# The recurrent layer's finish moved into the cross attention behind it, and batches 1 to 3 turned and projected between the first scores

## The reference, cut to what matters

```
xn = layernorm(x)
r  = scan_output(xn) + xn
x  = x + (layernorm(r) * gamma + beta)      # end of the recurrent sublayer
h  = layernorm(x)                           # x2 begins
q  = h @ Wq + bq ;  k, v = ctx @ Wk, ctx @ Wv ;  s = mask(q k^T / sqrt(8)) ...
```

## Time and profile before

| | |
|---|---|
| runs, median of 3 | 2433.44 us (2431.93 to 2447.59) |
| the profiled execution | 2440.75 us, its span 2438.9 us, mean granted TensorE clock 0.889 |
| PE matmul busy | 2066.0 us (85% of the span) |
| PE weight loads busy | 1383.0 us (57%) |
| DVE busy | 1662.4 us (68%) |
| ACT busy | 1045.7 us (43%) |
| POOL busy | 533.2 us (22%) |

### The profile page before, as it was taken

The page is one execution under the profiler, slowest core; times in us unless marked ns, Lnnn a source line. Parts: engine busy times, 40 slices in busy tenths (PEclk is TensorE's granted clock), DMA queues, the critical chain, the costliest instruction groups (busy, mean ns, idle before and its releaser), DMA issues. The chain is left out here.

```text
span 2438.9 us, 36556 instructions
## 1 busy us (share of the span) xinstructions
PE 2066.0 (85%) x12192; PEld 1383.0 (57%) x12216; DVE 1662.4 (68%) x4273; ACT 1045.7 (43%) x2326; POOL 533.2 (22%) x905
## 2 busy tenths in 40 slices
PE   6698899998999897767774997598699979999888
PEld 3455788884555455433332554587334348777777
DVE  5666677786675576779997565456679856666655
ACT  2354222222564453455551344322367734444333
POOL 0342110102110530068883321010211010000010
PEclk8698899997897799889996798799689979999989
DMA  8321000004120420000003220000511110000000
GB/s 338 99 60 23 1 1 1 1 1 130 44 53 18 121 60 2 1 1 0 1 1 105 73 48 8 1 1 1 174 36 46 33 44 1 1 1 1 1 1 18
DMA packets 60073, 94.61 MB, mean 39 GB/s; under 512 B 11313, under 2 KB 33137, under 8 KB 58737
## 3 DMA queue, kind: packets, MB, share of 16 engines
q1 hardware_dynamic: 29312, 55.29, 6.7%
q0 software_dynamic: 29952, 36.45, 6.2%
q10 hardware_dynamic: 624, 0.54, 0.1%
HBM read 65.50 MB, written 31.29 MB: 40 GB/s over the span
## 5 line engine op out<-in xcount | busy, mean ns | idle before, releaser
L1008 DVE TENSOR_REDUCE m<-banks 128x1 f32<-128x512 f32 (+3 forms) x512 | 272.6, 584 | 94.6 <-PE banks L1172 54.4
L2687 PEld LDWEIGHTS banks<-w_ffn,eh 128*128 128x128 f32 x2144 | 279.2, 191 | 23.5 <-DVE eh L2628 1.9
L2687 PE MATMUL banks<-w_ffn,eh 128*128 128x128 f32 x2144 | 281.2, 274 | 1.5 <-DVE eh L2628 1.5
L1140 ACT ACTIVATE p<-banks 128x512 f32<-128x512 f32 (+3 forms) x512 | 234.0, 522 | 101.4 <-PE banks L1218 58.7
L1443 DVE TENSOR_REDUCE m<-banks 128x2 f32<-128x308 f32 x384 | 165.7, 475 | 137.1 <-PE banks L1743 70.3
L2675 PE MATMUL banks<-x_hi,w_hi 128*128 128x512 f32 x472 | 211.2, 447 | 17.4 <-PEq L332 17.4
L1170 PE MATMUL banks<-K,Qf 32*128 32x512 f32 (+2 forms) x512 | 182.5, 515 | 14.6 <-PEq L332 9.9
L2657 ACT ACTIVATE et<-banks 128x512 f32<-128x512 f32 x140 | 83.6, 597 | 246.8 <-PE banks L2677 203.2
L2677 PE MATMUL banks<-x_hi,w_lo 128*128 128x512 f32 x472 | 188.7, 400 | 0.0
L2676 PE MATMUL banks<-x_lo,w_hi 128*128 128x512 f32 x472 | 187.6, 397 | 0.0
L1216 PE MATMUL banks<-Q,K 32*128 32x512 f32 (+2 forms) x512 | 153.5, 499 | 14.9 <-ACT p L1140 13.0
(11 more groups left out here) (423 smaller groups left out, 4332.7 us busy)
## 6 DMA issues: line engine op xcount, KB each, us to landing
Qf<-stack_q_plain POOLq DMA_DIRECT2D x48, 256.0 KB, 3.0
Qf<-stack_q_masked POOLq DMA_DIRECT2D x32, 256.0 KB, 3.0
K<-stack_k_self POOLq DMA_DIRECT2D x32, 256.0 KB, 3.1
w_ffn<-ffn_dram SPq DMA_DIRECT2D x1, 6144.0 KB, 35.2
stack_q_plain<-q_hi SPq DMA_DIRECT2D x24, 256.0 KB, 3.1
stack_q_masked<-q_hi SPq DMA_DIRECT2D x16, 256.0 KB, 3.0
stack_k_self<-k_hi SPq DMA_DIRECT2D x16, 256.0 KB, 3.8
K<-stack_k_ctx POOLq DMA_DIRECT2D x48, 80.0 KB, 2.7
```

Of the source, the lines that this page charges most:

```text
L1008: ins = dve.reduce_max(k.m[:, t, h:h + 1], bank[:, 0:(t + 1) * P if k.kind == "page" else S], AX)
L1140: nc.scalar.activation(k.p[:, x % PBUFS, q0:S], score_banks[x % 3][:, q0:S], ACT.Exp).then_inc(sem("exp_done"), 1)
L2687: last = pe.matmul(bank[:, t * P:(t + 1) * P], k.h[:, n % RING, t * P:(t + 1) * P], w(down.format(e))[:, i * P:(i + 1) * P], start=(i == 0 ...
```

## The change

The finish. `scan_finish` and its block are gone. x2 is called with `finish=True`, which counts as `early = 0`. POOL adds beta batch by batch at the start of the x2 block, ahead of its memsets. DVE multiplies by gamma and adds to x batch by batch (`add_scanned`), each time ahead of the norm of that batch; the norm of r of batch 3 stands between `add_scanned(2)` and `add_scanned(3)`.

The norms, in all three cross attentions. Only batches 0 and 1 are normed ahead of DVE's loop (in x1 the block before has normed 0 to 2). Batches 2 and 3 are normed in pieces in the loop: after `maximum(c)` for c = 1 to 6 the six pieces of batch 2, for c = 7 to 12 those of batch 3 (in x1 those of batch 3 for c = 1 to 6). `xn_ready` rises once for each batch.

PE. `normed(1)` and `project_queries(1)` are no longer ahead of the first scores. Batches 1, 2 and 3 are turned after c = 1, 7 and 13 and projected after c = 4, 10 and at the end of the 14 first scores, straight ahead of `lower_queries(0)`. POOL's low parts of queries 1 to 3 stand behind `load_stacks(2)`, and its first bias add waits for all four batches.

```diff
@@ -1365,15 +1365,14 @@
             self.rf = sb("rf", [P, KPAD])
 
 
-def cross_block(net, k, pre, scale):
+def cross_block(net, k, pre, scale, finish=False):
 
     nc, sem, ps, w = net.nc, net.sem, net.ps, net.w
     score_banks, first_banks = tuple(ps[n] for n in SBANKS), tuple(ps[n] for n in FBANKS)
     o_bank, misc = ps[5], ps[7]
     oT = net.xnT_all[:, 0:S]
     nch, nun = CCHUNKS, CUNITS
-    early = net.normed
-    all_normed = 1 if early else 2
+    early = 0 if finish else net.normed
     queries, keys = net.stack_q["masked" if k.masked else "plain"], net.stack_k["ctx"]
     kv_banks, x_banks, q_bank, bias_bank = (ps[0], ps[1]), (ps[2], ps[7]), ps[5], ps[4]
     mask_rows = {"row": 1, "add": 2, "full": 0}[k.kind]
@@ -1424,6 +1423,12 @@
                     ch.link(dve.memset(k.mrows[:, 1, :, S2:KPAD], 0.0))
                 dve.sem_inc(sem("mask_rows"), 1)
 
+            def add_scanned(b):
+                tiles, x = k.n.xn[:, b * QT:(b + 1) * QT, :], x_of(net, b)
+                ch.link(dve.tensor_tensor(tiles, tiles, over(w("m_gamma"), 1, QT), ALU.mult))
+                dve.wait_ge(sem("with_offset"), b + 1)
+                ch.link(dve.tensor_tensor(x, x, tiles, ALU.add))
+
             def masks(e):
                 kq = w("kq").rearrange("p (b k) -> p b k", b=B)
                 aq = w("aq").rearrange("p (t k) -> p t k", t=QT)
@@ -1474,6 +1479,8 @@
                 dve.tensor_tensor(x, x, misc[:].rearrange("p (t d) -> p t d", t=QT), ALU.add).then_inc(sem("x_added"), 1)
 
             dve.tensor_scalar(k.qs[:], w(f"{pre}_bq"), scale, None, ALU.mult).then_inc(sem("bias_ready"), 1)
+            if finish:
+                add_scanned(0)
             if not early:
                 vector_layernorm_of(dve, ch, net.x, k.n, 0, QT).then_inc(sem("xn_ready"), 1)
             dve.wait_ge(sem("row_done"), 1)
@@ -1482,13 +1489,26 @@
                 mask_rows_in()
             else:
                 masks(0)
-            vector_layernorm_of(dve, ch, net.x, k.n, max(early, 1) * QT, B * QT).then_inc(sem("xn_ready"), 1)
+            if finish:
+                add_scanned(1)
+                vector_layernorm_of(dve, ch, net.x, k.n, QT, 2 * QT).then_inc(sem("xn_ready"), 1)
+                add_scanned(2)
+                ch.link(vector_layernorm_of(dve, ch, k.n.xn, k.n, (B - 1) * QT, B * QT))
+                add_scanned(3)
+            elif early <= 1:
+                vector_layernorm_of(dve, ch, net.x, k.n, QT, 2 * QT).then_inc(sem("xn_ready"), 1)
+            begun = max(early, 2)
             done = 0
             for c in range(nch * LAST):
                 n, i = divmod(c, nch)
                 if k.kind == "full" and i == 0 and n % GROUPS == 1 and n // GROUPS + 1 < B:
                     masks(n // GROUPS + 1)
                 maximum(c)
+                b, piece = divmod(c - 1, PIECES)
+                if 0 <= b < B - begun:
+                    vector_norm_piece(dve, ch, net.x, k.n, (begun + b) * QT, (begun + b + 1) * QT, piece)
+                    if piece == PIECES - 1:
+                        dve.sem_inc(sem("xn_ready"), 1)
                 if n >= 2 * GROUPS and n % GROUPS < 3 and i in (3, 6):
                     e, piece = n // GROUPS - 2, 2 * (n % GROUPS) + i // 6
                     if piece == 0:
@@ -1558,6 +1578,10 @@
                     nc.gpsimd.tensor_copy(k.vr[rows, n % 2, RG * j:RG * j + HD], k.rests[rows, e, GROUP * g + j, :]).then_inc(sem("v_ready"), 1)
                 pool.wait_ge(sem("v_ready"), (n + 1) * (GROUP + 1))
 
+            if finish:
+                for b in range(B):
+                    x = x_of(net, b)
+                    nc.gpsimd.tensor_tensor(x, x, over(w("m_beta"), 1, QT), ALU.add).then_inc(sem("with_offset"), 1)
             pool.memset(k.K[:, :, KPAD:].bitcast(F32), 0.0).then_inc(sem("zeroed"), 1)
             pool.memset(k.mp[:].bitcast(F32), 0.0).then_inc(sem("zeroed"), 1)
             pool.memset(k.v[:], 0.0).then_inc(sem("zeroed"), 1)
@@ -1574,9 +1598,8 @@
                 low_keys(b)
             for n in range(2):
                 load_stacks(n)
-            low_queries(1)
             load_stacks(2)
-            for b in range(2, B):
+            for b in range(1, B):
                 low_queries(b)
             for n in range(LAST):
                 values(n)
@@ -1584,7 +1607,7 @@
                     load_stacks(n + 2)
                 if n < B:
                     if n == 0:
-                        pool.wait_ge(sem("xn_ready"), all_normed)
+                        pool.wait_ge(sem("xn_ready"), B - early)
                         pool.wait_ge(sem("row_ready"), 1)
                     x = x_of(net, n)
                     nc.gpsimd.tensor_tensor(x, x, over(k.bo[:], 1, QT), ALU.add).then_inc(sem("x_biased"), 1)
@@ -1715,7 +1738,7 @@
 
             def normed(b):
                 if b >= early:
-                    pe.wait_ge(sem("xn_ready"), 1 if b == 0 else all_normed)
+                    pe.wait_ge(sem("xn_ready"), b - early + 1)
                 if b >= 2:
 
                     pe.wait_ge(sem("xnT_ready"), b - 1)
@@ -1842,16 +1865,15 @@
             project_queries(0)
             for b in range(2, B):
                 keys_and_values(b)
-            normed(1)
-            project_queries(1)
             for c in range(nch + FIRST):
                 first_scores(c)
                 if k.kind == "full":
                     mask_first_scores(c)
-                if c in (2, 7):
-                    normed(2 + c // 7)
-                if c in (5, 10):
-                    project_queries(2 + c // 10)
+                if c in (1, 7, 13):
+                    normed(1 + c // 6)
+                if c in (4, 10):
+                    project_queries(1 + c // 6)
+            project_queries(B - 1)
             lower_queries(0)
             for m in range(LAST):
                 for s in range(4):
@@ -3066,28 +3088,6 @@
     end_of_block(net)
 
 
-def scan_finish(net, k):
-
-    sem, w = net.sem, net.w
-    with net.nc.Block() as block:
-
-        @block.gpsimd
-        def _(pool):
-            pool.tensor_tensor(net.x[:], net.x[:], over(w("m_beta"), 1, B * QT), ALU.add).then_inc(sem("beta_added"), 1)
-
-        @block.vector
-        def _(dve):
-            ch = Chain(dve, sem("dve_chain"))
-            xn = k.n.xn
-            ch.link(vector_layernorm(dve, ch, xn, xn, k.n, first=B - 1))
-            ch.link(dve.tensor_tensor(xn[:], xn[:], over(w("m_gamma"), 1, B * QT), ALU.mult))
-            dve.wait_ge(sem("beta_added"), 1)
-            ch.link(dve.tensor_tensor(net.x[:], net.x[:], xn[:], ALU.add))
-    end_of_block(net)
-
-
-
-
 def program(nc, x_dram, packs, out_dram):
     with ExitStack() as ctx:
         net = Net(nc, ctx)
@@ -3154,10 +3154,10 @@
                 k.more_buffers(net, sb)
                 narrow_block(net, k, pre)
 
-        def cross_attention(pre, kind):
+        def cross_attention(pre, kind, finish=False):
             stack, sb = scope()
             with stack:
-                cross_block(net, Cross(net, sb, kind), pre, 1.0 / float(np.sqrt(np.float32(HD))))
+                cross_block(net, Cross(net, sb, kind), pre, 1.0 / float(np.sqrt(np.float32(HD))), finish)
 
         class One:
             pass
@@ -3223,7 +3223,6 @@
                 scan_inputs(net, k, inner_sb)
             k.more_buffers(net, sb)
             scan_block(net, k)
-            scan_finish(net, k)
 
         def place_and_load(room, name, table):
             place(room, name, table)
@@ -3235,7 +3234,7 @@
 
         late_room, ffn2_room = ExitStack(), ExitStack()
         place_and_load(ffn2_room, "ffn2", FFN2)
-        cross_attention("x2", "full")
+        cross_attention("x2", "full", finish=True)
         wait_loaded("ffn2")
         experts("f2_router", route_sinkhorn, "relu", ("w{}", "d{}"), E8, 2, keep_x=True, norm_kind="double", ahead=2)
         ffn2_room.close()
```

## The result

The changed kernel takes 2455.45 us, the median of 6 runs (2444.17 to 2460.32), against 2434.53 us for the kernel before over the 6 runs beside it (2427.14 to 2447.59). The ratio is 1.0075 with a 95% interval of 1.0042 to 1.0109, so by the ratio it is 18 us slower (10 to 27). Forecast were 14 us more, 2447.4, with a range of 2431 to 2459.

The account below looks back on a forecast made before the run. The prediction took PE to bound the main loop, without slack to recover delays in the first scores. +12.2 (x0) + 6.5 (x1) - 4.7 (x2 with seam) = +14.0 us on the median 2433.44 gives 2447.4, range 2431 to 2459.

Parts of the forecast that it names:

- The seam: Between scan and x2: without the finish's block and its end, x2's first DVE operation starts 13.3 us earlier.
- x2's start: Head of x2: `add_scanned(0)` and POOL's beta adds start the norm of batch 0 4.0 us later (1.9 to 5.2).
- the 5.0: x2's start: if DVE and POOL take turns, the norm waits for three POOL adds and two DVE operations, 5.0 us.
- x0: First scores of x0: norm pieces between maxima and an uncovered tail make the Q copy 12.2 us later (+9 to +15).
- third count: x0: DVE's third count of `xn_ready`, after 7 maxima, 4.9 of pieces and 1.0 held, 8.8 us after the first maximum's start.
- fourth: x0: the fourth count of `xn_ready`, 8.9 us after the third, at 119.1; then a tail that nothing covers.
- x1: First scores of x1: c = 10 waits for the maximum of c = 7; Q copy +6.5 us (+4.7 to +7.2).
- rival B: First stages of x0, x1 and x2: PE's waits keep the granted clock low one stage more, adding 6 us; chance 0.18.
- x2: Seam and x2 together: of 13.3 us saved 8.6 are lost, Q copy 4.7 us earlier (ends -8 and -1).
- A: First scores: PE keeps the pace, pieces vanish in DVE's idle time; x0 +3, x1 +4, together -2.3 us; chance 0.13.
- C: x2: adds take turns in full, held operations double, x2 saves nothing; +18.7 us in all, 2452; chance 0.14.
- The sum: x0, x1 and x2 with its seam: +12.2 + 6.5 - 4.7 = +14.0 us; main forecast's chance 0.55.

Follow-up runs that it names:

- e4: Changed kernel, but POOL adds beta to all of x in one operation at the end of the scan block; 2449.64 us, ratio 1.0049.
- e3: Changed kernel, but in x0 and x1 DVE norms all batches ahead of the first scores, PE's new order kept; 2436.31 us, ratio 0.9999.
- e2: Changed kernel, but `scan_finish` is again in its own block and x2 is called without `finish`; 2456.51 us, ratio 1.0078.
- e6: Changed kernel, but x2 makes the masks of batch 1 at c = 16 and not at c = 8; 2458.18 us (one run).
- e7: Changed kernel, POOL's beta adds apart: first at x2's start, two behind the first queries' low part, fourth behind stage 2's loads; 2464.67 us (one run).
- e8: Changed kernel, but in x0 and x1 PE runs three unused matmuls ahead of each of the last two turns; 2452.75 us, ratio 1.0081.
- e10: Kernel before with finish and new scheme in x2 alone, beta in the scan inputs' block, batch 2 turned after c = 8; 2423.71 us, 0.9953.
- e1: Kernel before with the new scheme (finish inside, norm pieces, late turns) in x2 alone; 2432.2 us, ratio 0.9985.

## Why the prediction was right, and where it was off

The direction, the places and the waits were right, and the time lies in the range: forecast 2447.4 us, measured 2455.45. For the profiled execution the forecast of 2454.8 met 2455.34 by luck: the touched blocks grew by 19.1 us and not 14.0, and the untouched rest was 4.5 us shorter.

**The seam.** Forecast 13.3 us saved, measured 13.4 (257.17 to 243.80 in the windows).

**x2's start.** Forecast 4.0 us late out of 1.9 to 5.2, measured 5.3 (first load 16.93 to 22.19 us into the block), and e4 shows that 4.6 of it are POOL's adds. That they hold DVE was right. The way to the 5.0 was not, and that the size came near it is in part luck: the norm began behind two adds, not three, 3.1 us late (its first operation at 1326.00), and the other 2.2 us are the long `var`. It was held until 1329.74, though POOL's last add ended at 1327.96. I had also stepped back from the 5.0 to 4.0 without a row that asked for it.

**x0.** Forecast 12.2 us, measured 11.1 for the block. Step by step: third count 9.7 us after the first score (measured 9.4, the turn at 106.28), fourth 18.6 (18.0), Q copy 23.9 (23.2). PE idle 3.5 and 3.85 us with DVE as releaser, as said, and DVE busy for 15.6 of the 17.1 us from its first maximum to its last piece.

**x1.** Forecast 6.5 (4.7 to 7.2), measured 7.8 up to the Q copy and 10.9 for the block. This is the term that was mis-sized. Its steps held: c = 10 came 9.1 us after the first maximum (forecast 9.0) behind the maximum of c = 7, and the Q copy 8.7 us after that (forecast 8.2 at the low clock). One error is small: I chose 6.5 between the sums for the two clocks, and the granted clock was 0.50 for all of the 18.6 us. (The sum for the high clock, 1.1 + 0.5 + 3.8 behind 821.5, is also +4.4 and not the +4.7 written.) e3 shows besides that without the pieces 4.5 of the 7.8 remain, so PE's own order is a larger part of this stretch than the wait for DVE. The large error is that I counted nothing behind the Q copy, where x1 lost 3.4 us more, while its first score came 0.3 us earlier. Windows of the changed kernel, the 16 us behind the Q copy of x0 and x1:

```profile
120.09:136.09 16.00, 14.32 (x80) 7.76 (x80) 9.72 (x25) 8.60 (x17) 11.15 (x25) 0.78 0.38 101
...
836.03:852.03 16.00, 15.04 (x62) 8.70 (x62) 8.09 (x20) 7.20 (x14) 9.85 (x24) 0.54 0.35 92
```

and of the kernel before:

```profile
112.22:128.22 16.00, 14.51 (x72) 8.22 (x72) 8.34 (x23) 7.74 (x16) 11.12 (x25) 0.68 0.37 107
...
822.48:838.48 16.00, 14.39 (x71) 8.16 (x72) 8.17 (x23) 7.66 (x15) 10.90 (x25) 0.68 0.41 114
```

In x1 the mean granted clock of these 16 us is 0.54 where it was 0.68; PE is busy in both, but does 62 matmuls and not 71. This is what rival B describes, in one of the three places. Not all of the 3.4 us shows in other profiles: the four further kernels with this x1 (e2, e4, e6, e7) have blocks of 156.8 to 156.9 us, 1.5 less than the 158.4 here. This profile has a second stretch at 0.50, 3.4 us from 888.3 on, that those four lack. In x0 the clock was even better than before (0.78 against 0.68), which is in part why that block came out 1 us under its forecast. Over all profiles of x0 and x1 the long stretch at 1.00 begins 10.3 to 15.0 us behind the Q copy; in the changed x0, where it rose 10.5 to 14.9 us behind it, the blocks differ by 4.3 us. e8 didn't find what decides it, and it stays open.

**x2.** Forecast 4.7 us saved in seam and block, measured 2.9. The 1.8 that are missing are mainly the first score, which came 3.4 us later in the block and not 2.3, and 0.7 up to the Q copy, forecast at 28.3 us and measured at 29.0. I had drawn this stretch as bound by DVE behind the masks; by e6 and e10 neither engine bounds it alone.

**The rivals.** A (PE keeps the pace, the pieces vanish) is refuted by e3 for x0, where the pieces cost 9.9 us; its prices for the order alone, +3 and +4 in blocks, came near (e3: 4.7 and 3.1). B happened in x1. C (x2 saves nothing) did not: seam and x2 together are shorter than before by 2.9 us in the changed kernel and by 4.7 in e1.

**The sum.** +11.1, +10.9, -2.9 against +12.2, +6.5, -4.7. The direction and the places were right; the sum of the blocks was 5 us low (14.0 against 19.1), by what came behind the Q copy and the low clock in x1, and by x2's start.

The sentence of the Trainium skill (SBUF — State Buffer, section "Who interferes with whom") that the one that comes second is fully blocked agrees with the multiply of 1.55 us behind an add. The same section says that a VectorE operation in a 2-port mode contends with GpSimd, and names no exception there for a GpSimd operation that only writes. This case doesn't settle it: `var` was held beyond the last add until four of POOL's memsets were over (1329.71), but in the kernel before the same operation started while the same memsets ran (from 1312.93 to 1315.55) and was not held:

```profile
1314.36 0.17 DVE L371 TENSOR_SCALAR var<-aggr 128x4 f32<-128x4 f32 x1
```

## What to carry to other kernels

Work that is moved out of a free shadow (here the norm of two batches, under queries on their way to DRAM and back) into a loop in which two engines hand each other banks can cost its full length, even where the engine that takes it on was busy for only two thirds of the loop, if an in-order engine waits for its last piece: in x0 the 9.8 us of pieces cost 9.9. Move a step only in the place where the wait it removes ends last: the scheme of pieces and late turns cost 11.1 us in x0 and 10.9 in x1, where the first score waited for the load, and 3.0 in x2 (e2), where it waited for the norm and came 2.2 us sooner. It paid nowhere; what pays is the finish inside x2. The finish in x2 with the norms and turns as before was not run, and may be better than all kernels here. And a POOL operation with DVE beside it wants a place where DVE is idle, not where POOL is: the same beta add cost 4.6 us at x2's start (e4), 3.5 at the scan's end, and nothing in the inputs' block.

## What was not expected of the hardware

A chain of tiny operations feels a POOL operation in full: 2.42, 2.50 and 2.99 us for one `var` of 0.17. Matmuls put into waits raised the granted clock inside the stretch, but it was back at 0.50 before the Q copy; the block was as long as one without them. And blocks with identical code differ by up to 14.6 us between executions, more than any single term of this change.
